# Gate masks and weights on GpSimd, a mixed pair turned by feature halves, and new instruction orders on four engines

## The chip, the cores and the metric

One core of one Trainium2 chip runs the kernel. The metric is device microseconds of one execution; the median of three runs of the kernel before is 122.1 us.

## The reference

`x` is (32, 32, 512) float32: 32 samples of 32 tokens (channels) with 512 features. Two residual blocks follow each other.

```python
# block 1
att   = softmax(gelu(gelu(cond @ W0 + b0) @ W1 + b1) @ W2 + b2)          # (32, 8)
mixed = einsum('boi,bih->boh', einsum('bk,koi->boi', att, weight), x) + (att @ bias_k)[:, :, None]
q, k, v = bitnet_linear(mixed, ...)         # sign of the weight times a row scale, nan_to_num
out   = softmax(q k^T / 4) v                # 32 heads of 16, 8 key/value heads, 32 keys
x     = x + bitnet_linear(out, o_weight, o_scale)
# block 2
y      = conv1d(x, weight(32, 8, 9), groups=4) + cond @ c_weight.T + bias
logits = y @ router_w.T + router_b          # 8 experts
w      = the two largest probabilities, divided by their sum, scattered into (N, 8)
x      = x + einsum('ner,eor->no', einsum('nd,erd->ner', y, A) * w[:, :, None], Bm) * 0.5
```

## The kernel before

The 1024 rows (sample, token) are eight tiles of 128 rows and four pairs of tiles. All engines run at once, each through a written-out list of small functions; semaphores join them, and an engine that meets a wait holds everything behind it in its list.

For pair `i`: VectorE makes the mixing matrices (`mix_weights`, `sum_weights`), TensorE mixes (`mix_bias`, `mix`), VectorE turns the result (`turn_mixed(i)`, two transposes, one for each tile of the pair) and makes its low part (`low_part(i, b)`, `b` a half of the features), ScalarE its high part (`high_part(i, b)`), TensorE projects to queries, keys and values (`project_first` for pair 0, `project(i, b)` after), ScalarE scales (`scale_qkv`), VectorE guards (`guard_qkv`) and turns the values. For tile `t` and head half `h`: GpSimd spreads keys and values block-diagonally (`spread_keys`, `spread_values`), TensorE scores, VectorE takes maxima and shifts (`row_tops`, `shift_rows`), ScalarE exponentiates, VectorE sums and inverts, GpSimd multiplies (`normalise(t, h)`), TensorE turns (`turn_probs`), ScalarE copies (`copy_probsT`), TensorE attends and projects out (`attend`, `project_out`), VectorE scales (`scale_y`), GpSimd adds the residual (`residual(t)`, VectorE for tile 7), ScalarE issues the store to DRAM (`store_x1(t)`), and SyncE reads it back as a shifted window (`to_window(t)`). Then TensorE convolves and turns (`convolve`, `turn_conv`), VectorE adds the bias (`bias_conv`), TensorE multiplies by the expert and router matrix (`ffn_up(t)`).

The gate of tile `t`: VectorE adds the router bias and finds the two largest logits with their indices (`gate_top`, L1006 to L1011), makes the indices floats and compares them with 0 to 7 (`gate_masks`, L1015, L1017), ScalarE makes the exponential of the difference (`gate_exponent`), VectorE makes its sum with one, the weights `gate_w` and the inverse (`gate_weights`, L1024, L1026, L1029), and applies them (`gate_apply`, L1035). TensorE turns (`turn_gated`), ScalarE copies (`copy_gatedT`), TensorE multiplies down (`ffn_down`), VectorE finishes (`finish`, L1047), SyncE stores.

Beside these, `o_scales` (VectorE) makes the output scales, SyncE stores them to DRAM and spreads them back (`store_o_scale`, `spread_o_scale`), `sum_o_scales` (ScalarE) waits for that, `bound_on_output` (GpSimd, five 1x1 operations) waits for the sum, and `bound_o` (VectorE) loads the flag. `keep_busy` is a matmul whose result nobody reads.

Of the kernel before, what the change touches and what calls it, by code (L numbers as in the profile page):

```python
# [10 lines left out]
ALU = mybir.AluOpType  # L11
# [3 lines left out]
P = 128  # L15
# [49 lines left out]
def build(nc, cond_pack, misc, mix_w, mix_b, x_rows, qkvT, qkv_rows, woT, wo_rows, conv_w,  # L65
          ffn_in, ffn_out, out):
    with ExitStack() as ctx:
# [299 lines left out]
        def _(pool):  # L367
# [103 lines left out]
            spread_keys(1)  # L471
            clear_windows()
            spread_keys(2)
            normalise(0, 0)
            spread_keys(3)
            spread_values(0)
            normalise(0, 1)
            normalise(1, 0)
            spread_values(1)
# [3 lines left out]
            bound_on_output()  # L483
            spread_keys(5)
            normalise(2, 1)
            residual(0)
            normalise(3, 0)
            spread_values(2)
            spread_values(3)
            spread_keys(6)  # L490
            normalise(3, 1)
            normalise(4, 0)
            residual(1)
            clear_third()
            gather_taps()
            spread_values(4)
            spread_keys(7)
            normalise(4, 1)
            normalise(5, 0)
            residual(2)  # L500
            residual(3)
            normalise(5, 1)
            spread_values(5)
            normalise(6, 0)
            normalise(6, 1)
            normalise(7, 0)
            spread_values(6)
            spread_values(7)
            residual(4)
            residual(5)  # L510
            normalise(7, 1)
            residual(6)


        @block.scalar
        def _(act):
# [51 lines left out]
            def high_part(i, b):  # L568
                act.wait_ge(mixed_turned, 2 * i + 2)
# [62 lines left out]
            def gate_exponent(t):  # L632
                act.wait_ge(top_ready, t + 1)
                nc.scalar.activation(gate_e[:, t % 2, :], logit_top[:, t % 2, 0:1], ACT.Exp, bias=logit_top[:, t % 2, 1:2],
                                     scale=-1.0).then_inc(gate_exp, 1)
# [6 lines left out]
            turn_shares()  # L642
            sign_qkv(0)
            sign_qkv(1)
            sign_qkv(2)
            sign_qkv(3)
            high_part(0, 0)
            high_part(0, 1)
            sum_x(0)
            sum_x(1)  # L650
            high_part(1, 0)
            high_part(1, 1)
# [3 lines left out]
            sum_x(2)  # L656
            sum_x(3)
            scale_qkv(0, 0)
# [5 lines left out]
            sum_rows(BLOCKS + 0, 3)  # L664
            high_part(2, 0)
            high_part(2, 1)
            scale_qkv(1, 0)
            scale_qkv(1, 1)
            sign_wo(0)
            sum_rows(BLOCKS + 2, 4)  # L670
            sign_wo(1)
            scale_qkv(1, 2)
            scale_qkv(1, 3)
            scale_qkv(1, 4)
            scale_qkv(1, 5)
            exponents(0, 0)
            scale_qkv(2, 0)
            high_part(3, 0)
            scale_qkv(2, 1)
            high_part(3, 1)  # L680
            scale_qkv(2, 2)
            exponents(0, 1)
            exponents(1, 0)
            exponents(1, 1)
            scale_qkv(2, 3)
            scale_qkv(2, 4)
            keep_conv_bias()
            scale_qkv(2, 5)
            copy_probsT(0, 0)
            exponents(2, 0)  # L690
            copy_probsT(0, 1)
            sign_wo(2)
            exponents(2, 1)
            scale_qkv(3, 0)
            scale_qkv(3, 1)
            sign_wo(3)
            attn_high(0)
            copy_probsT(1, 0)
            sum_o_scales()
            copy_probsT(1, 1)  # L700
            exponents(3, 0)
            exponents(3, 1)
            scale_qkv(3, 2)
            scale_qkv(3, 3)
            scale_qkv(3, 4)
            scale_qkv(3, 5)
            copy_probsT(2, 0)
            store_x1(0)
            attn_high(1)
            copy_probsT(2, 1)  # L710
            exponents(4, 0)
            exponents(4, 1)
            copy_probsT(3, 0)
            attn_high(2)
            copy_probsT(3, 1)
            exponents(5, 0)
            store_x1(1)
            copy_probsT(4, 0)
            exponents(5, 1)
            attn_high(3)  # L720
            copy_probsT(4, 1)
            exponents(6, 0)
            exponents(6, 1)
            store_x1(2)
            attn_high(4)
            store_x1(3)
            copy_convT(0)
# [943 lines left out]
```

## Time and profile before

| | us |
|---|---|
| three runs | 121.7, 122.1, 124.11 |
| profiled execution, its own time | 121.39 |
| span of the profiled execution | 119.6 |
| busy: TensorE, VectorE, ScalarE, GpSimd | 105.5, 92.7, 62.7, 48.9 |
| idle of TensorE until the scores of the first conditioning layer, and from its last matmul on | 2.75, 3.2 |

The span lies inside the execution's own time and is 1.8 us shorter. The busy time of TensorE counts the drain of a matmul, so a wait shorter than that drain does not show as idle.

### The profile page before, as it was taken

How to read it: one execution, taken by the hardware profiler on the slowest of the kernel's cores; microseconds unless marked ns; L12 is line 12 of the kernel's file. 1: busy time of each engine (PE TensorE's matmuls, PEld its weight loads, DVE VectorE, ACT ScalarE, POOL GpSimd, SP SyncE). 2: the span in 40 equal slices, each digit the busy share in tenths (PEclk: the TensorE clock that was granted, in tenths of full speed). 3: DMA queues.
4: the chain of work that ended last, by engine and by line, in shares of the span. 5: the costliest groups of instructions: out<-in, count | busy, mean ns of one | idle time of the engine just before them, and what ended most of it. 6: DMA issues, size and time to landing. Idle time of an engine off the chain costs nothing. (4 is left out here: it accounts for less than half of the span.)

```text
span 119.6 us, 3340 instructions
## 1 busy us (share of the span) xinstructions
PE 105.5 (88%) x1264; PEld 78.0 (65%) x1264; DVE 92.7 (77%) x244; ACT 62.7 (52%) x138; POOL 48.9 (41%) x74
## 2 busy tenths in 40 slices
PE   0979999979999899996869999899999899988870
PEld 0766698769999798974748577475756645644510
DVE  0158998839989999959989999979757685857851
ACT  4549889967484859395646163735244004031400
POOL 1020910025018639879999939693721000000000
PEclk9999999999999999999999999999999999999999
DMA  3899999950000000200393883997299859997032
GB/s 86 262 313 413 427 374 428 401 181 3 0 5 1 0 0 0 93 0 30 119 196 104 172 180 121 212 189 144 88 256 194 130 194 212 189 258 289 35 134 103
DMA packets 19237, 19.54 MB, mean 163 GB/s; under 512 B 1684, under 2 KB 14868, under 8 KB 18836
## 3 DMA queue, kind: packets, MB, share of 16 engines
q1 hardware_dynamic: 18068, 17.22, 55.7%
q10 hardware_dynamic: 1152, 2.10, 4.8%
q8 instruction: 10, 0.16, 0.6%
q14 instruction: 7, 0.06, 0.2%
HBM read 15.12 MB, written 4.20 MB: 162 GB/s over the span
## 5 line engine op out<-in xcount | busy, mean ns | idle before, releaser
L434 POOL TENSOR_TENSOR probs<-probs,row_inv 128x512 f32<-128x512 f32 x16 | 16.8, 1052 | 5.3 <-DVE row_inv L970 3.8
L1321 PE MATMUL halves<-mixed_hi,qkv_sign 128*128 128x256 f32 x72 | 17.3, 285 | 0.0
L1322 PE MATMUL halves<-mixed_lo,qkv_sign 128*128 128x256 f32 x72 | 16.7, 277 | 0.0
L1321 PEld LDWEIGHTS halves<-mixed_hi,qkv_sign 128*128 128x128 f32 x72 | 13.5, 188 | 0.4 <-issue 0.2
L1399 PE MATMUL halves<-wo_sign,attn_hi 128*128 128x512 f32 x32 | 13.6, 425 | 0.0
L1322 PEld LDWEIGHTS halves<-mixed_lo,qkv_sign 128*128 128x128 f32 x72 | 13.5, 188 | 0.0
L416 POOL TENSOR_TENSOR keys_diag<-kv,keymask 128x512 f32<-128x512 f32 x8 | 8.8, 1107 | 10.9 <-DVE calm L935 10.7
L1399 PE MATMUL halves<-wo_sign,attn_lo 128*128 128x512 f32 x32 | 12.6, 392 | 0.0
L966 DVE TENSOR_REDUCE row_sum<-probs 128x16 f32<-128x512 f32 x16 | 10.6, 671 | 1.5 <-ACT probs L590 1.4
L452 POOL TENSOR_TENSOR x_all<-x_all,o_out 128x512 f32<-128x512 f32 x7 | 9.0, 1280 | 6.3 <-DVE o_out L983 6.3
L590 ACT ACTIVATE probs<-probs 128x512 f32<-128x512 f32 x16 | 9.8, 628 | 3.3 <-DVE probs L960 3.3
L960 DVE TENSOR_TENSOR probs<-halves,row_max 128x512 f32<-128x512 f32 x16 | 10.6, 682 | 0.6 <-PE halves L1370 0.3
L954 DVE TENSOR_REDUCE row_max<-halves 128x16 f32<-128x512 f32 x16 | 10.2, 665 | 0.5 <-PE halves L1347 0.4
L1452 PEld LDWEIGHTS halves<-ffn_in_sb,woT_sb 128*128 128x128 f32 x64 | 8.1, 190 | 3.8 <-issue 2.8
L1465 PE MATMUL halves<-ffn_out_sb,gatedT 128*128 128x512 f32 x16 | 8.9, 641 | 1.3 <-ACT gatedT L640 0.7
L640 ACT ACTIVATE gatedT<-halves 128x128 f32<-128x128 f32 x8 | 2.2, 277 | 14.3 <-PE halves L1458 14.3
L1452 PE MATMUL halves<-ffn_in_sb,woT_sb 128*128 128x136 f32 x64 | 8.9, 285 | 0.7 <-ACT gatedT L640 0.5
L1347 PE MATMUL halves<-keys_diag,queries 64*128 64x128 f32 x128 | 9.2, 282 | 0.1
L580 ACT ACTIVATE queries<-halves,scale_all 128x256 f32<-128x256 f32 x16 | 6.8, 469 | 3.4 <-PE halves L1322 3.4
L1347 PEld LDWEIGHTS halves<-keys_diag,queries 64*128 64x128 f32 x128 | 7.9, 188 | 1.0 <-issue 0.7
L1047 DVE SCALAR_TENSOR_TENSOR x_all<-halves,x_all 128x512 f32<-128x512 f32 x8 | 5.5, 688 | 3.9 <-PE halves L1465 3.9
L426 POOL TENSOR_TENSOR vals_diag<-values_t,valmask 128x512 f32<-128x512 f32 x8 | 8.4, 1059 | 0.0
(144 smaller groups left out, 223.4 us busy)
## 6 DMA issues: line engine op xcount, KB each, us to landing
rows_sb<-x_turned SPq DMA_DIRECT2D x18, 256.0 KB, 5.1
x_all<-in_x_rows SPq DMA_DIRECT2D x4, 512.0 KB, 9.1
x_turned<-x_all ACTq DMA_DIRECT2D x8, 256.0 KB, 2.5
out_rows<-x_all SPq DMA_DIRECT2D x8, 256.0 KB, 3.7
qkvT_sb<-in_qkvT SPq DMA_DIRECT2D x4, 384.0 KB, 5.9
rows_sb<-in_qkv_rows SPq DMA_DIRECT2D x1, 1536.0 KB, 9.8
qkv_sign<-x_turned SPq DMA_DIRECT2D x6, 256.0 KB, 5.2
rows_sb<-in_wo_rows SPq DMA_DIRECT2D x1, 1024.0 KB, 14.0
```

Source lines behind the costliest of these rows:

```text
L434: pool.tensor_tensor(probs[:, t % 2, h, :, :], probs[:, t % 2, h, :, :], row_inv[:, t % 2, h, :].unsqueeze(2).to_broadcast([P, HALF, TOKENS]),
L452: pool.tensor_tensor(x1[:, t, :], x_all[:, t, :], o_out[:, t % 2, :], ALU.add).then_inc(x1_ready, 1)
L590: nc.scalar.activation(probs[:, t % 2, h, :, :], probs[:, t % 2, h, :, :], ACT.Exp, scale=float(DIM) ** -0.5).then_inc(exp_ready, 1)
L954: v.tensor_reduce(row_max[:, t % 2, h, :], scores, AX_X, ALU.max).then_inc(max_ready, 1)
L960: v.tensor_tensor(probs[:, t % 2, h, :, :], scores, row_max[:, t % 2, h, :].unsqueeze(2).to_broadcast([P, HALF, TOKENS]), ALU.subtract).th ...
L966: v.tensor_reduce(row_sum[:, t % 2, h, :], probs[:, t % 2, h, :, :], AX_X, ALU.add).then_inc(sum_ready, 1)
L1321: mm(dst, w, mixed_hi[:, ph, cols(i % 2, PAIR)], start=(ph == 0 and n % 2 == 0), stop=False)
L1322: last = mm(dst, w, mixed_lo[:, ph, cols(i % 2, PAIR)], start=False, stop=(ph == PHASES - 1 and n % 2 == 1))
L1347: last = mm(ps_scores[h][:, s * P:(s + 1) * P], queries[rows, PER_TILE * t + s, :, :], keys_diag[rows, t % 2, s, :, :].rearrange("p g k -> ...
L1399: last = mm(ps_y[:, :], part[:, t % 2, j, :, :], wo_sign[:, j, :], start=(j == 0 and part is attn_hi), stop=(j == MEMBERS - 1 and part is ...
L1452: last = mm(ps_ffn(t)[:, 0:FFN_COLS], convT[t % 2][:, ph, :, :], ffn_in_sb[:, ph, :], start=(ph == 0), stop=(ph == PHASES - 1))
L1465: mm(ps_down[:, :], gatedT[:, t % 2, :], ffn_out_sb[:, :], start=True, stop=True).then_inc(ffn_done, 1)
```

## The change

Four things change. (1) `gate_masks(t)` moves to GpSimd and becomes four operations: indices to float, a mask for the first index, a mask for the second times `gate_e`, and their sum `gate_w`. VectorE keeps the sum and the inverse; `gate_apply` waits for GpSimd's `gate_w`. (2) `turn_mixed(i)` makes its two transposes by halves of the features instead of by tiles, and `high_part(i, b)` waits for its own half alone. (3) Some waits protect the shared buffers (`idx_f_ready` before `max_index`, `gate_mask_ready` before the exponential, `gated_ready` before `gate_w`). (4) The lists of TensorE, VectorE, ScalarE and GpSimd are in new orders; SyncE's is the same.

```diff
+            def gate_masks(t):
+                iota = misc_sb[:, MISC["iota"]]
+                pool.wait_ge(gate_idx_ready, t + 1)
+                pool.tensor_copy(gate_idx_f[:, t % 2, :], gate_idx[:, t % 2, 0:2]).then_inc(idx_f_ready, 1)
+                pool.wait_ge(idx_f_ready, t + 1)
+                pool.tensor_scalar(gate_mask[:, t % 2, 0, :], iota, gate_idx_f[:, t % 2, 0:1], None, ALU.is_equal).then_inc(gate_mask_ready, 1)
+                pool.wait_ge(gate_exp, t + 1)
+                pool.tensor_scalar(gate_mask[:, t % 2, 1, :], iota, gate_idx_f[:, t % 2, 1:2], gate_e[:, t % 2, :],
+                                   ALU.is_equal, ALU.mult).then_inc(gate_mask_ready, 1)
+                pool.wait_ge(gate_mask_ready, 2 * (t + 1))
+                reached(pool, gated_ready, t - 1)
+                pool.tensor_tensor(gate_w[:, t % 2, :], gate_mask[:, t % 2, 0, :], gate_mask[:, t % 2, 1, :],
+                                   ALU.add).then_inc(gate_w_ready, 1)
             def high_part(i, b):
-                act.wait_ge(mixed_turned, 2 * i + 2)
+                act.wait_ge(mixed_turned, 2 * i + b + 1)
             def turn_mixed(i):
-                for a in range(2):
-                    v.transpose(mixed[:, i % 2, :, cols(a, P)].rearrange("p k (q o) -> p q k o", q=PER_TILE),
-                                mixing(i)[:, :, cols(a, P)].rearrange("p q (k r) -> p q k r", k=PHASES)).then_inc(mixed_turned, 1)
+                for b in range(2):
+                    v.transpose(mixed[:, i % 2, 2 * b:2 * b + 2, :].rearrange("p k (a q o) -> p q a k o", a=2, q=PER_TILE),
+                                mixing(i).rearrange("p q (a k r) -> p q a k r", a=2, k=PHASES)[:, :, :, 2 * b:2 * b + 2, :]
+                                ).then_inc(mixed_turned, 1)
```

The parts of the new lists that matter below, in their order:

```
GpSimd   ... normalise(1,0) bound_on_output spread_values(2) normalise(1,1) spread_keys(4) ...
         ... residual(4) gate_masks(0) normalise(7,0) normalise(7,1) residual(5) gate_masks(1)
         gate_masks(2) residual(6) gate_masks(3) ... gate_masks(7)
ScalarE  turn_shares sum_x(0) sign_qkv(0) high_part(0,0) high_part(0,1) sign_qkv(1..3) sum_x(1) ...
         ... scale_qkv(1,0) scale_qkv(1,1) sum_rows(6) sum_rows(8) scale_qkv(1,2) ...
         ... copy_probsT(0,0) scale_qkv(2,4) scale_qkv(2,5) sum_o_scales copy_probsT(0,1) scale_qkv(3,0) ...
         ... copy_gatedT(1) gate_exponent(2) store_x1(6) copy_gatedT(2) copy_convT(3) store_x1(7) ...
VectorE  ... turn_mixed(2) low_part(1,0) sum_scales keep_scale_v low_part(1,1) bound_qkv sum_rows(7)
         guard_qkv(0) sum_rows(9) turn_mixed(3) low_part(2,0) o_scales row_tops(0,0) ...
         ... finish(3) bias_conv(6) bias_conv(7) finish(4) gate_top(6) gate_weights(6) gate_apply(6)
         finish(5) gate_top(7) gate_weights(7) gate_apply(7) finish(6) finish(7)
TensorE  ... turn_shares keep_busy(1) mix_bias(0) mix(0) mix(1) keep_busy x3 mix_bias(1) keep_busy(1) mix(2) mix(3)
         ... score(2) turn_probs(0,1) project(3,0) attend(0) score(3) turn_probs(1,0) project(3,1)
         turn_probs(1,1) project_out(0) turn_probs(2,0) score(4) attend(1) turn_probs(2,1) project(3,2)
         score(5) turn_probs(3,0) attend(2) turn_probs(3,1) project_out(1) attend(3) turn_probs(4,0) ...
         ... ffn_up(1) turn_probs(7,0) attend(6) turn_probs(7,1) turn_gated(1) convolve(3) attend(7)
         project_out(6) ffn_down(0) ffn_up(2) project_out(7) turn_conv(3) turn_gated(2) ffn_down(1)
         ffn_up(3) convolve(4) convolve(5) turn_conv(4) turn_conv(5) turn_gated(3) ffn_down(2) ...
```

Before, `o_scales` stood behind `row_tops(1,1)`, `sum_o_scales` behind `copy_probsT(1,0)`, `low_part(1,0)` behind `mix_weights(3)`, `attend(0)` behind `project(3,1)`, `project(3,2)` ahead of `turn_probs(1,1)`, `turn_gated(1)` behind `turn_conv(2) project_out(6) turn_probs(7,1)`, `residual(6)` was GpSimd's last, `store_x1(6)` stood behind `copy_gatedT(2)`, and `ffn_down(1)` between `convolve(5)` and `turn_conv(4)`.

## Rows read from the trace of the kernel before

**Rows 1.** Part 1 of the page: busy time, share, instructions.
```profile
PE 105.5 (88%) x1264; PEld 78.0 (65%) x1264; DVE 92.7 (77%) x244; ACT 62.7 (52%) x138; POOL 48.9 (41%) x74
```
**Rows 2.** Busy time in four stretches (length, each engine, clock, DMA share, GB/s).
```profile
25.00:46.00 21.00, 20.50 (x214) 19.40 (x213) 18.63 (x39) 13.64 (x31) 9.44 (x13) 1.00 0.05 12
46.00:72.50 26.50, 24.02 (x358) 18.29 (x357) 23.96 (x49) 15.02 (x30) 22.71 (x29) 1.00 0.43 101
72.50:95.00 22.50, 21.19 (x232) 14.05 (x229) 17.67 (x55) 9.73 (x21) 11.86 (x11) 1.00 0.94 177
95.00:117.20 22.20, 19.08 (x123) 9.86 (x123) 15.94 (x63) 4.99 (x15) 0.00 (x0) 1.00 0.73 179
```
**Rows 3.** Waits of TensorE: total us, times, longest.
```profile
PE halves L1370 <- POOL probs L434: 1.6, 2, 1.3
PE halves L1370 <- ACT probsT L597: 1.0, 1, 1.0
```
**Rows 4.** Groups by line: total busy us, mean ns.
```profile
L828 DVE STREAM_TRANSPOSE mixed<-halves 128x512 f32<-128x512 f32 x8 | 5.2, 687 | 1.0 <-PE halves L1289 1.0
L946 DVE STREAM_TRANSPOSE values_t<-kv 128x128 f32<-128x128 f32 x4 | 1.2, 288 | 0.0
```
**Rows 5.** Timeline of the head: start us, length us.
```profile
8.60 1.24 PE L1280 MATMUL halves<-attT,mix_b_wide 32*128 32x256 f32 x8 [0.27 <-ACT attT L544]
11.22 1.65 PE L1235 MATMUL halves<-cond_sb 128*128 128x128 f32 x6
...
23.01 0.68 DVE L834 TENSOR_TENSOR mixed_lo<-mixed,mixed_hi 128x512 fp32r<-128x512 f32 x1
```
**Rows 6.** Timeline of the output scales: SyncE's queue, ScalarE.
```profile
37.42 0.38 SPq L321 DMA_DIRECT2D o_scale_row<-scale_all  x1
46.47 0.33 SPq L326 DMA_DIRECT2D o_scale_bc<-o_scale_row  x1
50.43 0.63 ACT L606 ACTIVATE junk_o<-o_scale_bc 1x512 f32<-1x512 f32 x1 [1.02 <-DMA o_scale_bc<-o_scale_row]
```
**Rows 7.** Timeline of TensorE: `turn_probs(0,1)`, then `project(3,1)`, then `attend(0)`.
```profile
43.65 0.60 PE L1360 MATMUL halves<-misc_sb,probs 128*128 128x128 f32 x4
...
46.02 1.08 PE L1386 MATMUL halves<-probsT,vals_diag 64*32 64x128 f32 x32
```
**Rows 8.** Timeline of GpSimd in `bound_on_output`, each operation waiting for the last.
```profile
51.59 0.19 POOL L444 TENSOR_TENSOR bound<-bound 1x1 f32<-1x1 f32 x1
51.85 0.18 POOL L446 TENSOR_TENSOR bound<-bound 1x1 f32<-1x1 f32 x1
```
**Rows 9.** Timeline of VectorE in the gate of tile 7, and the end.
```profile
112.73 0.17 DVE L1006 TENSOR_TENSOR logits<-halves,misc_sb 128x8 f32<-128x8 f32 x1 [0.20 <-PE halves L1452]
...
113.41 0.17 DVE L1015 CAST gate_idx_f<-gate_idx 128x2 f32<-128x2 uint32 x1
...
114.21 0.35 DVE L1035 SCALAR_TENSOR_TENSOR gated<-halves,gate_inv,gate_w 128x128 f32<-128x128 f32 x1
...
116.48 0.69 DVE L1047 SCALAR_TENSOR_TENSOR x_all<-halves,x_all 128x512 f32<-128x512 f32 x1 [1.32 <-PE halves L1465]
```
**Rows 10.** Timeline of GpSimd and of VectorE in the gate of tile 0.
```profile
80.44 1.31 POOL L452 TENSOR_TENSOR x_all<-x_all,o_out 128x512 f32<-128x512 f32 x1
80.71 1.05 DVE L1015 CAST gate_idx_f<-gate_idx 128x2 f32<-128x2 uint32 x1
```
**Rows 11.** Timeline: `residual(6)`, `store_x1(6)` and `(7)`, `ffn_up(3)`.
```profile
88.84 1.27 POOL L452 TENSOR_TENSOR x_all<-x_all,o_out 128x512 f32<-128x512 f32 x1 [2.26 <-DVE o_out L983]
94.86 1.75 ACTq L630 DMA_DIRECT2D x_turned<-x_all  x2
...
95.27 1.17 PE L1452 MATMUL halves<-ffn_in_sb,woT_sb 128*128 128x136 f32 x8 [0.46 <-ACT gatedT L640]
```
**Rows 12.** Timeline of GpSimd: the masks of the heads, each independent.
```profile
12.65 0.65 POOL L399 TENSOR_TENSOR keymask<-misc_sb 128x4 f32<-128x4 f32 x1
13.25 0.35 POOL L402 TENSOR_TENSOR valmask<-misc_sb 128x4 f32<-128x4 f32 x2
```

More of the change, by code:

```diff
@@ L642, in _ @@
             turn_shares()
+            sum_x(0)
             sign_qkv(0)
+            high_part(0, 0)
+            high_part(0, 1)
             sign_qkv(1)
@@ L1475, in _ @@
             turn_shares()
+            keep_busy(1)
             mix_bias(0)
@@ L1503, in _ @@
             project(1, 2)
+            conv_context()
+            score(1)
             project(2, 0)
-            score(1)
             project(2, 1)
             project(2, 2)
-            conv_context()
+            turn_probs(0, 0)
             score(2)
-            turn_probs(0, 0)
+            turn_probs(0, 1)
             project(3, 0)
-            turn_probs(0, 1)
-            project(3, 1)
             attend(0)
@@ L1516, in _ @@
             turn_probs(1, 0)
-            project(3, 2)
+            project(3, 1)
             turn_probs(1, 1)
             project_out(0)
+            turn_probs(2, 0)
             score(4)
-            turn_probs(2, 0)
             attend(1)
             turn_probs(2, 1)
+            project(3, 2)
+            score(5)
             turn_probs(3, 0)
-            score(5)
-            project_out(1)
             attend(2)
             turn_probs(3, 1)
+            project_out(1)
+            attend(3)
             turn_probs(4, 0)
+            project_out(2)
             score(6)
-            attend(3)
-            project_out(2)
+            turn_probs(4, 1)
             convolve(0)
-            turn_probs(4, 1)
-            project_out(3)
             attend(4)
             turn_probs(5, 0)
+            turn_conv(0)
+            project_out(3)
             score(7)
-            turn_conv(0)
-            project_out(4)
             turn_probs(5, 1)
@@ L1543, in _ @@
             turn_probs(6, 0)
+            turn_probs(6, 1)
             attend(5)
-            turn_probs(6, 1)
+            project_out(4)
             turn_conv(1)
             ffn_up(0)
+            convolve(2)
             project_out(5)
+            turn_gated(0)
+            turn_conv(2)
+            ffn_up(1)
+            turn_probs(7, 0)
             attend(6)
-            turn_probs(7, 0)
-            turn_gated(0)
-            convolve(2)
-            ffn_up(1)
-            turn_conv(2)
-            project_out(6)
             turn_probs(7, 1)
@@ L1559, in _ @@
             attend(7)
+            project_out(6)
+            ffn_down(0)
             ffn_up(2)
+            project_out(7)
             turn_conv(3)
-            ffn_down(0)
-            project_out(7)
             turn_gated(2)
+            ffn_down(1)
             ffn_up(3)
@@ L1567, in _ @@
             convolve(5)
-            ffn_down(1)
             turn_conv(4)
+            turn_conv(5)
             turn_gated(3)
-            turn_conv(5)
             ffn_down(2)
@@ L1574, in _ @@
             ffn_up(5)
+            ffn_down(3)
             convolve(6)
-            ffn_down(3)
             turn_gated(4)
+            turn_gated(5)
+            ffn_down(4)
             turn_conv(6)
-            ffn_down(4)
+            convolve(7)
             ffn_up(6)
-            convolve(7)
-            turn_gated(5)
             turn_conv(7)
```

293 lines of the change are left out of this document (140 added, 153 removed).

## The prediction

> **What bounds the kernel now.** I read the busy shares first: TensorE is busy for 88% of the span and VectorE for 77% [rows 1]. A share is an average, so the stretches come next [rows 2]. From 25 to 46 us TensorE idles 0.5 us in 21, and VectorE 2.4. From 46 to 72.5 us TensorE idles 2.5 us in 26.5, VectorE as much, GpSimd 3.8: three engines are near their limit at once, and any hand-over can stall the next. From 72.5 to 95 us TensorE idles 1.3 us, VectorE 4.8. From 95 us on, TensorE idles 3.1 in 22.2 us and VectorE 6.3: there the latency of one tile's chain counts, not throughput. So the most that new orders can win is what TensorE idles: 7.4 us in these four stretches. The waits say where some of it sits: two for GpSimd's `normalise`, 1.6 us together, one for ScalarE's `copy_probsT`, 1.0 us [rows 3]. The chain that ended last could be followed for 2.5% of the span only, so I walked each engine's new list by hand, each step as long as its row, and noted at marks how late TensorE is against before for the same work done. The profiled execution took 121.39 us, 0.7 below the median of 122.1; the sum is made against it, and I keep its 1.8 us outside the span.
>
> **Head, +0.6 us at `project(1,0)`.** The feature halves let `high_part(0,0)` start one transpose (0.69 us, rows 4) earlier. That wins nothing: `project_first` stands behind `mix(3)` in TensorE's list. If the new pattern of the transposes ran at the rate of the 128x128 one, a quarter of the size in 0.29 us, one would take 1.15 instead of 0.69, eight of them 3.7 us of VectorE [rows 4]. I take 0.69, because the nearest row is the same operation on the same 128x512 elements out of the same banks; the bounds are 0 and +3.7. One `keep_busy` now stands between `turn_shares` and `mix_bias(0)`, one between `mix_bias(1)` and `mix(2)`. Three of them took 1.65 us, so each is 0.55 [rows 5]. The first fills a wait of 0.27 us that TensorE had there [rows 5] and costs the rest, 0.28. The second replaces one that stood between `mix(3)` and `project_first`: nothing. Then `low_part(1,0)` (0.68 us, rows 5) stands in VectorE's list ahead of `keep_scale_v`, in place of two small sums of some 0.1 each that move away; `total_bound` waits for `keep_scale_v`, and `mix(6)`, `project(1,0)` stand behind it: half of the difference is covered by `mix_bias(3)`, +0.3. ScalarE does `sum_x(0)` while it would otherwise wait for weights, and comes to `scale_qkv(0,0)` 1.7 us later; its consumers have 2 us. Nothing.
>
> **Output scales, +1.15 us at `attend(0)`.** `o_scales` moves up, from 37.3 to 31.2 us by my walk (it needs `sum_rows(6)` and `(8)` of ScalarE, which follow `project(1,0)`). Its way through DRAM is long: 9.05 us from the first issue to the second [rows 6], and 3.96 more to ScalarE's sum [rows 6], 13.0 in all. It comes back at 44.3. But `sum_o_scales` moves up too, ahead of `copy_probsT(0,1)`, and ScalarE's list stops there. The sum (0.63 and an accumulator read) and the copy (0.6) end at 45.8, and `attend(0)` needs the copy. TensorE is there at 44.65, because `project(3,1)` is no longer ahead of `attend(0)`; before, that project and a `turn_probs` filled 2.4 us [rows 7]. It waits 1.15 us. Behind ScalarE's stopped instruction stand `scale_qkv(3,0)` and `exponents(2,0)` as well. Lateness now 1.75. This stall can be from 0 (if the DMA is 1.2 us faster) to 2.2 us (if the scales are 1 us later).
>
> **The middle, -1.95 us up to `score(7)`.** `project(3,2)` now comes behind `turn_probs(2,1)`, and `score(5)` ahead of `turn_probs(3,0)`: that is work in the place where TensorE waited 1.3 and 1.0 us [rows 3]. My walk finds each `normalise`, each copy and each key spread ready when TensorE comes, but five of them by 0.3 us or less. I take all of that gain, 1.95 us of the 2.5 that stand there [rows 2]; the bounds are 0 and 2.5. TensorE is then 0.2 us ahead of before.
>
> **Gate on GpSimd.** On VectorE three operations go: from the cast to `gate_apply` was 0.80 us [rows 9], of which the sum and the inverse stay, so about 0.45 us of its time for each tile, 3.6 us in all. VectorE had idle time in those stretches [rows 2], so this is worth little in itself. GpSimd's small dependent operations start 0.26 us apart [rows 8]. Four, with the hand-over both ways, make 1.15 us from index to `gate_apply` instead of 0.80: +0.35 us of latency per gate, 2.3 from the logits to `turn_gated` instead of 1.9. In the masks of the heads single GpSimd operations lasted 0.65 [rows 12]; with that price the four take 2.6 us and a gate +1.8. I take 0.26, the row with dependent operations of a few elements; the bounds are 0 (the operations overlap) and +1.8.
>
> One more row speaks for the change: in the gate of tile 0 the cast took 1.05 us instead of 0.17, and ended with GpSimd's `residual` of 80.44 us [rows 10]. That 0.9 us goes with the cast, but VectorE waited for nothing that TensorE needed at once, so I count it at nothing. The Trainium skill ("SBUF — State Buffer", Who interferes with whom) says that a cast can take the port pair that VectorE shares with GpSimd, and that whichever started first blocks the other fully; the row agrees, 80.71 + 1.05 = 81.76 against 80.44 + 1.31 = 81.75. The Trainium skill ("GPSIMD Engine Reference", Engine selection) advises against GpSimd for two-input elementwise work, as about twice as slow; by that rule the three moved operations would cost some 0.6 us more per gate, an estimate, instead of 0.35, and with it at the same three places the sum would end 0.7 higher.
>
> Where the latency shows. `turn_gated(1)` had `turn_conv(2)`, `project_out(6)` and `turn_probs(7,1)` between it and its `ffn_up`; now two turns and one `attend`, 1.45 us of work against 2.3 of latency: +0.85. In the remainder of that stretch the walk is 0.05 better, lateness 0.6 at the end of `project_out(7)`. Next, `residual(6)` now stands behind `gate_masks(2)` in GpSimd's list. Before it was done at 90.1 [rows 11]; now it waits for the indices of tile 2 and ends 3.1 us after `ffn_up(2)`, at 95.9. `store_x1(6)` waits for it, and behind it in ScalarE's list stand `copy_gatedT(2)` and `copy_convT(3)`, which `ffn_up(3)` needs: a wait of 0.7 us, in place of the 0.46 it had [rows 11] less what the new order would have saved of it, +0.4. Lateness 1.0. The store itself goes from 94.9 [rows 11] to 95.95, still in time for `convolve(6)`. `convolve(5)` to `turn_conv(5)` loses its cover, `ffn_down(1)`: +0.3; up to `ffn_up(7)` the walk wins 0.15. Then the end: the last gate is 0.35 longer, and `gate_apply(6)`, held by `gate_masks(6)`, keeps `finish(5)` and `gate_top(7)` behind it in VectorE's list 0.6 us past the end of `ffn_up(7)`; before, `gate_top(7)` was there and waited for it [rows 9]. +0.95.
>
> **Sum.** 0.6 + 1.15 - 1.95 + 0.8 + 0.4 + 0.3 - 0.15 + 0.95 = +2.1. The last `finish` would start at 118.6 instead of 116.5 [rows 9]. 121.4 + 2.1 = 123.5 us.
>
> **The rivals.** *Even:* the output scales come back in time, or the last gates overlap better: without the 1.15 and half of the 0.95 it is 121.9; band 120.7 to 122.3. For it: that stall hangs on one DMA time seen once. *The orders pay:* no new stalls, and the waits of the tail go too: 0.6 of the head, less 2.5 of the middle and 0.5 of the wait at `ffn_up(3)`, less some VectorE time that matters: 121.4 - 2.4 = 119.0; band 118.4 to 120.4. For it: nearly every wait of rows 3 has its work moved. Against it: `store_x1(6)` and `turn_gated(1)`, whose places need no price. *Slower by the masks:* GpSimd's four operations take 0.65 each. A gate costs +1.8 instead of +0.35, 1.45 more, at `turn_gated(1)`, at `store_x1(6)` and in the last gate, three places that nothing covers: 123.5 + 4.3 = 127.8; band 125 to 128. It decides from about 0.4 us per operation. *Slower in the transposes or by missed hand-overs:* the five near ones miss by 0.3 each, or the transposes take part of their +3.7: 124.8 to 126.5. *The halves do nothing* is part of the forecast already.
>
> **How the numbers follow.** Forecast band (122.3 to 124.6): 0.42. Even: 0.25. The orders pay: 0.15. Masks: 0.12. Transposes and hand-overs: 0.06. The forecast is the likeliest. 2% is about what a measurement of this kernel can tell from no change: 119.7 and 124.5 around 122.1. Faster takes most of the third case, 0.13; slower the last two and a tenth of the forecast band, with a little of what lies over it, 0.24; within 2% the remaining 0.63. The range leaves out a tenth at each end: 120.0 to 126.0. The case bands of both signs hold most of the chance, so the likeliest's own range is 122.3 to 124.6.
>
> **What the profile after would show.** Right: ScalarE's `junk_o` waiting for `o_scale_bc` at about 44 us with TensorE's `attend(0)` idle before it; the cast and three operations in GpSimd's rows, 1.1 us from first to last; waits of TensorE at `turn_gated(1)` on `gated`; `store_x1(6)` near 96 us; `gate_top(7)` starting 0.6 us after `ffn_up(7)`; the two waits of rows 3 gone. Wrong: transposes of over 0.8 us; GpSimd masks of 0.65; `attend(0)` without a wait; or TensorE stalls between 46 and 72 us, which would mean that my walk, with five hand-overs within 0.3 us, was too kind.

## The result, and the profile after

Four executions of the changed kernel took 125.64, 126.54, 124.47 and 123.58 us, median 125.06; four of the kernel before beside them had a median of 122.01. The ratio is 1.0163, 95% interval 1.0124 to 1.0203: slower, by 2.0 us. Ratios leave out executions more than 1.5% above the fastest of their kernel, here two of the four, while medians are of all, so the two need not agree. In a second measurement, beside three of the experiments, the median was 125.29 against 121.59, ratio 1.027 [1.0217, 1.0323], from five executions of six. The sign is the same in both; the sizes are 1.6 and 2.7%, and the first rests on two executions.

The profiled execution took 125.64 us with a span of 123.7. First the busy shares and the granted clock of its page.

```profile
PE 108.1 (87%) x1264; PEld 79.0 (64%) x1264; DVE 89.0 (72%) x220; ACT 62.6 (51%) x138; POOL 57.8 (47%) x106
...
PEclk9999999999999999999999999999999999999955
```

Against [rows 1] VectorE has lost 3.7 us of work and 24 instructions, GpSimd has won 8.9 us and 32. The last two slices run at half of the clock, of which more below. Next come the same four stretches as in [rows 2].

```profile
25.00:46.00 21.00, 19.86 (x242) 18.22 (x241) 19.55 (x44) 15.18 (x38) 11.24 (x16) 1.00 0.10 28
46.00:72.50 26.50, 25.83 (x380) 20.64 (x380) 24.75 (x55) 16.86 (x32) 22.82 (x27) 1.00 0.41 91
72.50:95.00 22.50, 20.11 (x218) 13.48 (x214) 15.03 (x41) 8.13 (x17) 12.12 (x20) 1.00 0.82 162
95.00:117.20 22.20, 18.76 (x130) 9.60 (x129) 12.60 (x46) 5.41 (x15) 6.63 (x22) 1.00 0.80 183
```

The first number is the length, the second TensorE's busy time; their difference is its idle time. Before it was 0.5, 2.5, 1.3 and 3.1 us; now it is 1.1, 0.7, 2.4 and 3.4, and the span ends 4.1 us later. The middle has won 1.8 us, and the stretches around it have lost more. (A stretch of time doesn't hold the same work in both kernels; a comparison of the same work follows the experiments.) The waits of TensorE say to what.

```profile
PE halves L1463 <- DVE gated L1048: 2.0, 4, 1.0
PE halves L1375 <- ACT probsT L619: 1.1, 2, 0.9
...
PE halves L1457 <- ACT woT_sb L643: 0.9, 1, 0.9
PE halves L1365 <- ACT probsT L623: 0.8, 1, 0.8
PE halves L1420 <- DMA rows_sb<-x_turned: 0.6, 1, 0.6
```

The two waits of [rows 3] are gone. In their place stand `turn_gated` waiting for `gate_apply` (four times, up to 1.0 us), `turn_probs(6,1)` and `turn_probs(7,1)` each behind a copy of ScalarE, `ffn_up(3)` behind `copy_convT(3)`, and `convolve(1)` behind its window. None of the four is `turn_gated(1)`. The chain of the page that ended last gives TensorE 54% of the span, VectorE 18%, DMA 9%, GpSimd and ScalarE 4% each: no single culprit.

The groups of VectorE show the new transposes, 694 ns each instead of the 687 of [rows 4].

```profile
L851 DVE STREAM_TRANSPOSE mixed<-halves 128x512 f32<-128x512 f32 x8 | 5.2, 694 | 2.1 <-PE halves L1294 2.1
```

The timeline, place by place (start, length, engine; the idle time before it in brackets): the output scales and `attend(0)`; `residual(6)`, `turn_gated(2)`, `store_x1(6)`, `ffn_up(3)`; and the gate of tile 7 to the end.

```profile
30.95 0.38 SPq L321 DMA_DIRECT2D o_scale_row<-scale_all  x1
...
40.47 0.33 SPq L326 DMA_DIRECT2D o_scale_bc<-o_scale_row  x1
...
44.68 0.63 ACT L628 ACTIVATE junk_o<-o_scale_bc 1x512 f32<-1x512 f32 x1 [1.88 <-DMA o_scale_bc<-o_scale_row]
...
45.98 0.67 PE L1391 MATMUL halves<-probsT,vals_diag 64*32 64x128 f32 x32 [0.45 <-issue]
...
95.22 1.27 POOL L466 TENSOR_TENSOR x_all<-x_all,o_out 128x512 f32<-128x512 f32 x1
...
95.70 0.33 PE L1463 MATMUL halves<-misc_sb,gated 128*128 128x128 f32 x1 [0.22 <-DVE gated L1048]
...
96.51 0.33 ACTq L652 DMA_DIRECT2D x_turned<-x_all  x1
...
97.76 0.50 PE L1457 MATMUL halves<-ffn_in_sb,woT_sb 128*128 128x136 f32 x2 [0.86 <-ACT woT_sb L643]
...
115.39 0.15 DVE L1030 TENSOR_TENSOR logits<-halves,misc_sb 128x8 f32<-128x8 f32 x1
...
116.08 0.19 POOL L453 CAST gate_idx_f<-gate_idx 128x2 f32<-128x2 uint32 x1 [1.60 <-DVE gate_idx L1036]
...
116.37 0.31 POOL L455 TENSOR_SCALAR gate_mask<-misc_sb,gate_idx_f 128x8 f32<-128x8 f32 x1
116.66 0.40 POOL L457 TENSOR_SCALAR gate_mask<-misc_sb,gate_idx_f,gate_e 128x8 f32<-128x8 f32 x1
117.15 0.20 POOL L461 TENSOR_TENSOR gate_w<-gate_mask 128x8 f32<-128x8 f32 x1
117.38 0.35 DVE L1048 SCALAR_TENSOR_TENSOR gated<-halves,gate_inv,gate_w 128x128 f32<-128x128 f32 x1 [0.93 <-POOL gate_w L461]
...
117.79 0.33 PE L1463 MATMUL halves<-misc_sb,gated 128*128 128x128 f32 x1 [1.04 <-DVE gated L1048]
...
118.48 2.07 PE L1470 MATMUL halves<-ffn_out_sb,gatedT 128*128 128x512 f32 x2 [0.37 <-ACT gatedT L663]
120.59 0.69 DVE L1060 SCALAR_TENSOR_TENSOR x_all<-halves,x_all 128x512 f32<-128x512 f32 x1 [2.26 <-PE halves L1470]
```

Read the gate first. From the cast to `gate_apply` it is 1.30 us where VectorE took 0.80 [rows 9]; GpSimd's three followers start 0.29, 0.29 and 0.49 us behind one another, and VectorE waits 0.93 us for `gate_w`. `ffn_up(7)` had ended at 114.77; its logits are read at 115.39 only, because `gate_apply(6)` and `finish(5)` stood ahead. The last `ffn_down` takes 2.07 us; with the full clock it takes 1.12 (below). The cast of tile 0, blocked for 0.9 us before [rows 10], is now on the engine that had blocked it and takes 0.19 (at 80.99 us).

### The profile page after: what moved, and what is told of

Its sections match the earlier page's. It is cut to its first block, busy times and chain, and to the rows that moved or that the text cites. A ratio compares the mean times of both kernels' runs of the same rounds, so it can differ in the third digit from the quotient of the medians.

```text
span 123.7 us, 3366 instructions
## 1 busy us (share of the span) xinstructions
PE 108.1 (87%) x1264; PEld 79.0 (64%) x1264; DVE 89.0 (72%) x220; ACT 62.6 (51%) x138; POOL 57.8 (47%) x106
## 4 chain that ended last, share of the span: by engine, by line
PE 54%; DVE 18%; DMA 9%; issue 6%; POOL 4%; ACT 4%; SPq 1%; ACTq 0%; POOLq 0%; DVEq 0%
PE halves L1404 8%; PE halves L1308 5%; PE halves L1352 5%; DMA qkv_sign<-x_turned 4%; PE halves L1420 4%; PE halves L1470 4%; PE halves L1294 4%; PE halves L1457 4%; DMA x_turned<-x_all 3%; PE halves L1326 3%; PE halves L1327 3%; PE halves L1285 3%; DVE mixed_lo L858 3%; DVE row_max L978 3%; DVE probs L984 3%
## 5 line engine op out<-in xcount | busy, mean ns | idle before, releaser
L1326 PE MATMUL halves<-mixed_hi,qkv_sign 128*128 128x256 f32 x72 | 17.7, 289 | 0.2 <-DVE mixed_lo L858 0.2
L453 POOL CAST gate_idx_f<-gate_idx 128x2 f32<-128x2 uint32 x8 | 1.5, 186 | 21.8 <-DVE gate_idx L1036 21.5
L426 POOL TENSOR_TENSOR vals_diag<-values_t,valmask 128x512 f32<-128x512 f32 x8 | 8.9, 1114 | 4.9 <-DVE values_t L972 4.3
L1470 PE MATMUL halves<-ffn_out_sb,gatedT 128*128 128x512 f32 x16 | 9.5, 677 | 1.1 <-ACT gatedT L663 1.1
L619 ACT ACTIVATE probsT<-halves 128x512 f32<-128x512 f32 x8 | 4.8, 597 | 7.2 <-PE halves L1375 5.8
```

The costliest lines, as they stand in the source:

```text
L426: pool.tensor_tensor(vals_diag[:, t % 2, :, :, :].rearrange("p s a (b d) -> p (s a) b d", d=DIM), values.unsqueeze(2).to_broadcast([P, 2 * ...
L1326: mm(dst, w, mixed_hi[:, ph, cols(i % 2, PAIR)], start=(ph == 0 and n % 2 == 0), stop=False)
L1470: mm(ps_down[:, :], gatedT[:, t % 2, :], ffn_out_sb[:, :], start=True, stop=True).then_inc(ffn_done, 1)
```

## The experiments

The forecast was a sum of stalls by place. Two ways of reading the result are to be told apart. One: the two parts, orders and masks, add up, and the masks cost where a gate's latency is bare. The other: each stall of the new orders that the trace shows costs its own length, so mending it gives that length back. Ratios are to the kernel before, in executions of the same chip.

**The masks alone.** The orders, transposes and lists of before; only `gate_masks` goes to GpSimd.

```diff
 residual(4)                      # GpSimd's list of before
+gate_masks(0)
 residual(5)
 normalise(7, 1)
+gate_masks(1)
 residual(6)
+gate_masks(2) ... gate_masks(7)
```

> The kernel before in its own orders, with only the gate's masks and weights on GpSimd. Theory M (the masks' latency is the cost): each gate 0.35 us longer, at the last gate and wherever nothing covers it, so 0.4 to 1.5 us slower than before (ratio 1.003 to 1.012), the four GpSimd operations about 1.1 us from first to last. Theory O (the new orders are the cost, the masks are harmless or help by the 0.45 us per tile that VectorE gains): within 0.3 us of before, or up to 1 us faster.

Median 123.95 us, ratio 1.0177 [1.0122, 1.0232]. Waits of VectorE and of TensorE in its trace:

```profile
DVE gated L1047 <- POOL gate_w L461: 5.7, 6, 1.0
```
```profile
PE halves L1462 <- DVE gated L1047: 1.4, 2, 1.0
```

The first line is the new one: 0.95 us of VectorE at each of six gates. The masks alone make the kernel slower, by 2.1 us, more than the 0.4 to 1.5 that were expected. Its trace also holds a wait of 1.97 us and a fall of the clock at 58 to 63 us, ahead of the first gate, which the masks can't have made.

**The orders alone.** The changed kernel with `gate_masks` and `gate_weights` on VectorE as before.

```diff
             gate_top(7)          # VectorE's list of after
+            gate_masks(7)
             gate_weights(7)      # and so for each tile
```

> The changed kernel with the masks back on VectorE, just ahead of gate_weights; halves and new orders stay. Theory M: most of the loss is gone, ratio to before 0.99 to 1.005. Theory O: it stays slow, 1.01 to 1.02, with store_x1(6) about 1.2 us earlier (residual(6) no longer behind the masks of tile 2) but with the waits for the output scales at attend(0) and for the windows as they are.

Median 123.03 us, ratio 1.0082 [1.0033, 1.0131]: the orders alone lose 1.0 us, between what the two theories expected. Its last gate, to be held against the one above:

```profile
115.14 0.17 DVE L1016 CAST gate_idx_f<-gate_idx 128x2 f32<-128x2 uint32 x1
...
115.95 0.35 DVE L1036 SCALAR_TENSOR_TENSOR gated<-halves,gate_inv,gate_w 128x128 f32<-128x128 f32 x1
```

0.81 us from the cast to `gate_apply`. 1.8% and 0.8% make 2.6%: what the second measurement of the changed kernel gave (2.7%), and more than the first did (1.6%).

**The halves alone.** The kernel before with the new `turn_mixed` and `high_part`.

> The kernel before with only the transposes of a mixed pair split by feature halves, and each high part waiting for its own half. Forecast of the record: nothing is gained, since project_first stands behind mix(3); the transposes last 0.69 us as before: ratio 0.997 to 1.003. Rival: the new pattern is slower (over 0.8 us each), which gives 1.005 or more; or the high parts that start 0.65 us earlier save time at project(1,0), 0.995 or less.

Median 121.83 us of 12 executions, ratio 1.0022 [0.9994, 1.0050]. The transposes by their group:

```profile
L828 DVE STREAM_TRANSPOSE mixed<-halves 128x512 f32<-128x512 f32 x8 | 5.2, 689 | 1.6 <-PE halves L1290 1.6
```

689 ns: the pattern is free, and the earlier start wins nothing that the runs can tell.

**A busy tail.** The changed kernel with nine matmuls that nobody reads around the last two gates, to hold the clock.

```diff
 turn_gated(6)
+stay_busy(2)
 ffn_down(6)
+stay_busy(5)
 turn_gated(7)
+stay_busy(2)
 ffn_down(7)
```

> The changed kernel with nine matmuls that nobody reads between the last turns and the last ffn_down, where TensorE waits for the gates. Theory C (in the changed kernel the clock falls to half in the last 5 us in some executions, because TensorE waits longer there, and this costs about 1 us when ffn_down(7) takes 2.08 instead of 1.12 us): the granted clock stays at 1.0 to the end in every execution, no execution of 125 us and over, median 123.5 to 124. Rival (the fall is not tied to what TensorE does in the tail): the low clock shows again in some executions, and the added matmuls change nothing or cost 0.2 us.

Median 125.06 us, ratio 1.0323 [1.0276, 1.0369]. The last `ffn_down`:

```profile
118.39 1.12 PE L1475 MATMUL halves<-ffn_out_sb,gatedT 128*128 128x512 f32 x2
```

The granted clock was 1.0 to the end and the matmuls took 1.12 instead of 2.07 us, but so they did without the filler in every other trace, the changed kernel's second one among them. The fall ahead of the last `ffn_down` belongs to that one execution and explains 0.95 us of its span. The expectation failed: two of the six executions had a mean clock of 0.984 and 0.985 in spite of the filler, three took over 125 us, and one of those, of 125.99 us, had the full clock. So the clock doesn't explain the median.

**The scales' sum later.** `sum_o_scales` behind `attn_high(0)` on ScalarE, `bound_on_output` behind `normalise(2, 0)` on GpSimd: the stall that the forecast priced highest is taken away.

```diff
 scale_qkv(2, 5)
-sum_o_scales()
 copy_probsT(0, 1)
 ...
 attn_high(0)
+sum_o_scales()
```

> The changed kernel with sum_o_scales back behind attn_high(0) in ScalarE's list and bound_on_output behind normalise(2,0) in GpSimd's. The record's step: ScalarE stopped for the output scales holds attend(0); in the trace of the changed kernel TensorE stood there about 0.45 us. Theory S (that stall carries to the end): the wait before attend(0) goes, 0.4 to 1.1 us faster than the changed kernel, ratio to before 1.007 to 1.013. Theory A (later waits, for the window of tile 1 and for copies of probsT, absorb it): attend(0) starts 0.4 us or more earlier, but the ratio stays at 1.014 to 1.019.

Median 125.15 us, ratio 1.0318 [1.0276, 1.0359]. TensorE and VectorE in its timeline:

```profile
44.91 0.67 PE L1391 MATMUL halves<-probsT,vals_diag 64*32 64x128 f32 x32
46.26 0.90 PE L1352 MATMUL halves<-keys_diag,queries 64*128 64x128 f32 x11 [0.69 <-DVE calm L959]
...
53.28 0.69 DVE L1007 TENSOR_TENSOR o_out<-halves,o_scale_bc 128x512 f32<-128x512 f32 x1 [1.43 <-POOL safe_flag L448]
...
57.33 0.94 PE L1352 MATMUL halves<-keys_diag,queries 64*128 64x128 f32 x12 [0.59 <-DVE probs L984]
```

`attend(0)` starts without a wait, 1.1 us earlier than in the changed kernel's trace; 0.6 of that is this execution's head (`project(1,0)` at 25.39 instead of 25.96), and 0.5 is the wait. But `score(3)` right behind waits 0.69 us for VectorE (by the profile, for `guard_qkv(1)`). The two lines below are from the busy tail, whose lists up to there are those of the changed kernel.

```profile
45.48 0.67 PE L1396 MATMUL halves<-probsT,vals_diag 64*32 64x128 f32 x32
46.83 1.16 PE L1357 MATMUL halves<-keys_diag,queries 64*128 64x128 f32 x16 [0.68 <-DVE calm L959]
```

There too `attend(0)` doesn't wait, and so in every trace of the new orders but the changed kernel's first. `score(3)` starts 20.86 to 20.99 us behind `project(1,0)` in all of them, with that stall (20.86) and without. So the stall cost nothing, because VectorE's work for `score(3)` ends last. The edit isn't a clean test of the rest, though: `bound_on_output` comes later with it, VectorE waits 1.43 us for its flag, and `score(5)` waits 0.59 us for VectorE. From `project(1,0)` to `project_out(3)` the three kernels with this edit take 44.1 us, the other traces of the new orders 43.2 to 43.4: the edit costs 0.8 us of its own.

**`residual(6)` first.** It goes ahead of `gate_masks(2)` in GpSimd's list.

> The changed kernel with residual(6) ahead of gate_masks(2) on GpSimd. The record's step: residual(6) behind the masks stops ScalarE at store_x1(6), and ffn_up(3) waits. Theory S: ffn_up(3) no longer waits 0.86 us for copy_convT(3), 0.5 to 0.9 us faster than the changed kernel, ratio to before 1.009 to 1.012. Theory A (the rest is bound by the gates' latency, so the time comes back as waits for the gates): the wait goes but the ratio stays at 1.014 to 1.019.

Median 124.86 us, ratio 1.0286 [1.0244, 1.0328]. Timeline of TensorE at `ffn_up(3)`:

```profile
97.85 1.20 PE L1457 MATMUL halves<-ffn_in_sb,woT_sb 128*128 128x136 f32 x8
```

The wait of 0.86 us is gone: from `ffn_up(2)` to `ffn_up(3)` it takes 4.73 us instead of 5.61. The time is no better than the changed kernel's by more than the runs can tell (124.9 against 125.1). But the trace says what became of the gain: it is still there at the last gate (`turn_gated(2)` and `turn_gated(7)`).

```profile
96.67 0.33 PE L1463 MATMUL halves<-misc_sb,gated 128*128 128x128 f32 x1 [0.21 <-DVE gated L1048]
...
117.86 0.33 PE L1463 MATMUL halves<-misc_sb,gated 128*128 128x128 f32 x1 [1.04 <-DVE gated L1048]
```

That is 21.2 us from the one to the other, where the changed kernel takes 22.1 (95.70 to 117.79). What this execution won there it had lost before: `project_out(4)` ran at half of the clock and took 3.3 us instead of 2.1. Four of the six executions had a mean clock as low as this one's (0.975 to 0.977); whether that ate the gain in them too isn't shown.

**All mended, with either engine for the masks.** The head's `keep_busy` as before, both edits above, `residual(2)` ahead of `spread_values(5)`, and `attend(5)` between `turn_probs(6,0)` and `(6,1)`; once with the masks on GpSimd, once on VectorE.

> The changed kernel with five places mended: the two keep_busy back where they were, sum_o_scales and bound_on_output as in e5, residual(6) as in e6, residual(2) ahead of spread_values(5), and attend(5) between turn_probs(6,0) and turn_probs(6,1). If the stalls that the orders make are what costs: about 2 us faster than the changed kernel, ratio to before 0.995 to 1.005. If GpSimd's gate latency is what costs: still 1.008 to 1.015, with the last gates unchanged (0.9 us of VectorE idle before gate_apply(7)).

> The same five places mended in the kernel with the new orders and the masks on VectorE (residual(6) needs none there). If both the orders' stalls and GpSimd's latency cost, this is the fastest: ratio to before 0.985 to 1.0. If the mends win nothing because later waits absorb them, it stays at the 1.008 of the orders alone.

Masks on GpSimd: median 125.74 us, ratio 1.0321 [1.0268, 1.0374]. On VectorE: 123.54 us, 1.0174 [1.0135, 1.0213]. Neither is better than its parent (125.1 and 123.0), and the second is worse than the orders alone (1.0082, in another set of executions) by more than the intervals. Between the two the ratios differ by 1.5%, 1.8 us, again for the masks. The traces say why nothing came back: the edit for the sum costs its 0.8 us in both (`score(5)` waits 0.66 and 0.64). In the first, the 0.9 us of `residual(6)` are won, but `convolve(2)` waits 1.8 us for its window, and `project_out(5)` behind it takes 3.4 us at half of the clock. The late window isn't new with these edits: it cost 1.3 us in the orders alone and 1.55 with the head restored.

**The changed kernel again, and three more.** The first is the second measurement quoted above. The tail on VectorE: tiles 3 to 7 have their masks and weights on VectorE, tiles 0 to 2 on GpSimd. The head restored: the three `keep_busy` where they were. The swap: `attend(5)` between the two `turn_probs` alone.

```diff
 gate_top(3)                      # VectorE's list, tiles 3 to 7
-gate_weights(3)
+tail_masks(3)                    # gate_masks as before, counted by two
+tail_weights(3)                  # gate_weights as before
```

> The changed kernel once more, beside the three others and the kernel before on one chip. If the ratio of the first measurement (1.016) holds, the part for the orders (0.8%) and the part for the masks (1.8% in before's orders) do not add up, or only partly. If those two parts add up, the ratio is 1.025 to 1.03, some 124.5 to 125 us, as the other versions built on it showed.

> The changed kernel with the masks and weights of tiles 3 to 7 made by VectorE again, those of tiles 0 to 2 still by GpSimd. Theory (latency of the last gates): from 95 us on each tile waits for its gate, so this takes back most of what the masks cost: 1.5 to 2 us less than the changed kernel, the last gate_apply some 0.5 us behind the index of tile 7 nearer to it (0.85 instead of 1.36), and no wait of VectorE on gate_w. Rival (the cost lies in the first gates and in GpSimd's residual and stores before 95 us): no more than 0.6 us less. Rival (the clock falls whenever TensorE has idled, whoever makes the masks): the time stays within 0.5 us.

> The changed kernel with the three keep_busy of the head back where they were before. The forecast priced them at 0.28 us at project(1,0). Theory: project_first and project(1,0) start 0.3 to 0.5 us earlier, and the gain is absorbed before 46 us by the wait for the output scales, so the time is within 0.3 us of the changed kernel. Rival: the head sets the pace of everything behind it, and the time falls by 0.5 us or more. Second rival: keep_busy in the wait holds the clock up, and without it the head gets slower, by 0.5 us or more.

> The changed kernel with attend(5) between turn_probs(6,0) and turn_probs(6,1) on TensorE, as cover for ScalarE's copy. The changed kernel idles 0.87 us there. Theory: that wait goes (0.6 to 0.9 us in place), and the chain of tiles 2 and 3 behind it, which waits for VectorE and ScalarE, takes most of it back: 0 to 0.4 us less. Rival: each idle of TensorE counts in full: 0.8 us less.

| | median us | ratio |
|---|---|---|
| again | 125.29 | 1.0270 [1.0217, 1.0323] |
| tail on VectorE | 124.83 | 1.0276 [1.0231, 1.0322] |
| head restored | 125.13 | 1.0270 [1.0223, 1.0316] |
| swap | 125.23 | 1.0187 [1.0138, 1.0236] |

The head restored: no gain, as the theory said, but not for its reason. `project(1,0)` doesn't start earlier; it starts 18.8 us behind `turn_shares`, against 18.2 in the changed kernel's first trace and 18.9 in its second. The swap: its median is the changed kernel's, and the means of the six executions are 125.0 and 125.2; its ratio is better, at the edge of the intervals, and I take it for no gain shown. With it `turn_gated(7)` starts at 117.91 us against 117.79. It is still the useful trace, since its clock stayed at 0.999: the timeline of its last two steps, then the same in the tail on VectorE.

```profile
113.79 1.09 PE L1457 MATMUL halves<-ffn_in_sb,woT_sb 128*128 128x136 f32 x8
...
117.91 0.33 PE L1463 MATMUL halves<-misc_sb,gated 128*128 128x128 f32 x1 [1.05 <-DVE gated L1048]
```
```profile
114.62 1.09 PE L1475 MATMUL halves<-ffn_in_sb,woT_sb 128*128 128x136 f32 x8
...
117.86 0.33 PE L1481 MATMUL halves<-misc_sb,gated 128*128 128x128 f32 x1 [0.55 <-DVE gated L1061]
```

From `ffn_up(7)` to `turn_gated(7)` it takes 4.12 us with GpSimd's masks and 3.24 with VectorE's; the orders alone had 3.17. So 0.9 us in the last gate is shown in place. But the time did not follow: 0.46 us of the medians and nothing of the ratio, where 1.5 to 2 were expected. In that trace `project_out(4)` took 3.4 us instead of 2.1, at half of the clock; of the other executions only the mean clock is recorded (0.985 to 1.0, 0.986 here).

**The same work in every trace.** From `turn_gated(2)` to `turn_gated(7)` all kernels do the same work on TensorE, and behind `turn_gated(7)` each trace has 4.98 us left (the changed kernel's first has 5.93, by the fall of its clock). First the two ends in the kernel before, then, with `ffn_up(3)` between them, in the orders alone.

```profile
94.54 0.27 PE L1458 MATMUL halves<-misc_sb,gated 128*128 128x128 f32 x1
...
114.62 0.33 PE L1458 MATMUL halves<-misc_sb,gated 128*128 128x128 f32 x1 [0.33 <-DVE gated L1035]
```
```profile
96.01 0.33 PE L1459 MATMUL halves<-misc_sb,gated 128*128 128x128 f32 x1 [0.15 <-DVE gated L1036]
...
97.19 1.19 PE L1453 MATMUL halves<-ffn_in_sb,woT_sb 128*128 128x136 f32 x8
...
116.36 0.33 PE L1459 MATMUL halves<-misc_sb,gated 128*128 128x128 f32 x1 [0.48 <-DVE gated L1036]
```

| us from start to start | `turn_gated(2)` to `ffn_up(3)` | to `ffn_up(7)` | to `turn_gated(7)` | all |
|---|---|---|---|---|
| before | 0.73 | 16.33 | 3.02 | 20.1 |
| masks alone | 0.73 | 16.99 | 3.77 | 21.5 |
| orders alone, and mended with VectorE's masks | 1.18 | 16.0 | 3.17 | 20.35 |
| changed kernel (twice), head restored, sum later, busy tail, swap | 2.06 | 15.9 | 4.11 | 22.1 |
| `residual(6)` first, and all mended | 1.18 | 15.9 | 4.10 | 21.2 |
| tail on VectorE | 2.06 | 16.45 | 3.24 | 21.75 |

Traces of one kind agree within 0.03 us here. The orders cost 0.3 us in this part, and the masks in the new orders 1.8: 0.9 at `ffn_up(3)`, because `residual(6)` stands behind `gate_masks(2)`, and 0.9 in the last gate. This also says why the tail on VectorE won little: it kept `residual(6)` behind `gate_masks(2)`, lost 0.5 us more in the middle column (`turn_conv(5)` and `turn_gated(4)` wait longer), and had only the last gate to win.

## Why the prediction was right

It gave 123.5 us, with 120.0 to 126.0 and the chance on "within 2%". Measured: 125.06 in the first set, a ratio of 1.016. The sign and the range hold, though the second measurement, 1.027, lies over 2%; the likeliest's own band of 122.3 to 124.6 was left by 0.5 us on the upper side. In the changed kernel's first trace, same work against same work, the parts of the sum come out so. (`score(3)` is compared without `project(3,1)`, 2.01 us, and `score(7)` without `turn_conv(0)`, 0.41, which the two lists put on different sides.)

| TensorE's lateness gained | forecast | measured |
|---|---|---|
| up to `project(1,0)` | +0.6 | +0.44 |
| to `score(3)` | +1.15 | +1.37 |
| to `score(7)` | -1.95 | -1.99 |
| to `turn_gated(2)` | +0.8 | +1.33 |
| to `turn_gated(7)` (0.4 + 0.3 - 0.15 + 0.95) | +1.5 | +2.01 |
| sum | +2.1 | +3.2 |

The middle was right, and the rest was priced low by 1.1 us in all. The forecast of 2.1 us agrees with the first measurement (2.0), but not with the second (3.3) nor with this sum, so the close fit to the first ratio is partly luck. By its steps:

- *Head, +0.6.* Measured 0.44 at `project(1,0)` (25.52 to 25.96 us), but that can't be told from chance: with the same head it starts 17.4 to 18.9 us behind `turn_shares` in eight traces, against 17.7 before. Restoring it gave nothing back, in place or in time.
- *Transposes.* 694 ns, as taken; the price of +3.7 us from the small pattern fell. The halves alone: 1.0022.
- *Output scales, +1.15 at `attend(0)`.* The stop of ScalarE is there: 13.7 us from the first issue (30.95) to the sum (44.68), forecast 13.0, and `attend(0)` at 45.98 against 45.8. But TensorE came 0.9 us later than in my walk and waited 0.45 instead of 1.15, in this trace and in no other. The lateness at `score(3)`, near the forecast in size, has another cause: `score(3)` waits for VectorE, with the stall at `attend(0)` or without it. The step was wrong in its mechanism, and its size came out near by luck.
- *Middle, -1.95.* 1.99 from `score(3)` to `score(7)`, TensorE's idle 0.7 instead of 2.5 us: right, and the largest term.
- *Gate, +0.35.* 0.50 measured (1.30 less 0.80, cast to `gate_apply`). The price of 0.26 us per operation came from a chain of 1x1 operations; here the cast of 128x2 and the first mask are followed after 0.29 each, and the operation that compares and multiplies after 0.49. The rival price of 0.65 fell. The three operations that left VectorE were busy 0.57 us there by the sum of their rows, and GpSimd's four are 1.10. The Trainium skill ("GPSIMD Engine Reference", Engine selection) has GpSimd about twice as slow for elementwise work with two inputs; 1.9 times is near that, but it compares four operations with three others, and the one two-input operation among GpSimd's took 0.20 us, so the rule itself isn't tested. The +0.6 worked out from it was nearer than my +0.35. The Trainium skill ("Perfetto Trace Analysis", GPSIMD Engine Instruction) says to time GpSimd by the spacing of starts and not by the spans; so read, the four steps from the cast make 1.30, where the spans sum to 1.10.
- *`turn_gated(1)`, +0.85.* The wait for the gate that this step forecast is not there: TensorE's wait on that row is 0.02 us, and at most 0.2 in any trace. `turn_probs(7,1)` just ahead of it waits 0.77 us for `copy_probsT`, and 0.58 in the orders alone, whose masks are VectorE's. So little of the lateness there is the masks'. The other lateness of this stretch comes from two hand-overs that the walk counted as met: `turn_probs(6,1)` straight behind `(6,0)` waits 0.9 for `copy_probsT`, `convolve(1)` 0.6 for its window.
- *`residual(6)` behind `gate_masks(2)`, +0.4.* As forecast to the place: ended 96.49, store at 96.51, `ffn_up(3)` waits 0.86 (0.7 forecast). Mended, it gives 0.9 us back as far as the last gate in both traces, though the times don't show it. The term was half of that.
- *End, +0.95.* `gate_top(7)` 0.62 us behind the end of `ffn_up(7)`, 0.6 forecast. The rest of the difference at `turn_gated(7)`, 117.79 where the sum gives 116.7 (114.62 + 2.1), is what came before plus the gate's 0.15. The last `finish` stood 0.95 us later again, by the clock of that execution.

So the terms that were mis-sized are those of the masks behind `turn_gated(2)`: they cost 1.8 us in place, half of it through `residual(6)` (0.9 for a term of 0.4) and half in the last gate (0.9 more than with VectorE's masks, where the latency alone was priced at 0.35). The step that was wrong in its mechanism is the output scales, and with it the forecast of a wait on the gate at `turn_gated(1)`. By the times the masks alone cost 2.1 us, and the ratios of the changed kernel and of the orders alone differ by 1.9%, 2.3 us. The orders alone lost 1.0. What the whole adds up to, 2.0 or 3.3 us, the two measurements leave open; the parts, and the traces with their 3.2, speak for the larger.

The walk by places treated each stall as lasting and as its own. The runs show two kinds. The stall at `attend(0)` cost nothing, since another wait ended later right behind it. The one at `ffn_up(3)` lasted to the end.

Not settled: the 0.5 to 0.9 us by which the times put the masks above what the traces show in place (1.8 in the new orders, 1.4 in those of before), and why the times of `residual(6)` first and of the tail on VectorE don't follow their traces. The falls of the clock in the middle of some executions are a candidate that no run tests. No version beat the kernel before, and the best of the changed ones, the halves apart, was the orders with VectorE's masks, 0.8% slower.

## What to carry to other kernels

Moving small dependent operations to an idle engine is paid in latency: 0.46 us of VectorE's busy time was freed per tile (3.7 us over eight), and the chain that everybody waited for became 0.5 us longer, in a stretch where VectorE idled anyway. The idle engine's own list counts too: a residual that stood behind the moved operations cost as much again. Count such a move by the chain's latency and by what queues behind it, and not by the busy shares. Before a stall is priced at its length, look at the next wait of the same engine: where that one ends later whatever you do, as at `score(3)`, the stall is worth nothing. And when times scatter by more than the effect, compare the time between the same two instructions, with the same work between them, in several traces; here it agreed within 0.03 us in six traces whose spans differ by up to 2.9.

## What was not expected of the hardware

The granted clock of TensorE fell from 2.4 to 1.2 GHz for a few microseconds in the middle of some executions, and matmuls took half as long again or more: `project_out` 3.55 us instead of 2.12 in the masks alone, 3.4 instead of 2.1 with the tail on VectorE, the last `ffn_down` 2.07 instead of 1.12 in the changed kernel. Five of the fourteen traces have such a fall between 58 and 87 us, each behind waits of TensorE. With `residual(6)` first the waits were those of `convolve(1)` and `turn_probs(6,1)`; the third line is the stretch behind them, granted clock 0.50:

```profile
72.86 1.07 PE L1420 MATMUL halves<-rows_sb,conv_w_sb 96*32 96x512 f32 x8 [0.77 <-DMA rows_sb<-x_turned]
...
75.19 0.46 PE L1375 MATMUL halves<-misc_sb,probs 64*128 64x64 f32 x8 [0.87 <-ACT probsT L619]
```
```profile
76.00:79.00 3.00, 3.00 (x30) 2.13 (x15) 1.77 (x4) 1.87 (x4) 1.11 (x2) 0.50 1.20 214
```

Such waits are not enough, though: the busy tail, whose lists are the same up to there, had nearly the same two, and kept the full clock.

```profile
73.34 1.07 PE L1425 MATMUL halves<-rows_sb,conv_w_sb 96*32 96x512 f32 x8 [0.74 <-DMA rows_sb<-x_turned]
...
75.67 0.46 PE L1380 MATMUL halves<-misc_sb,probs 64*128 64x64 f32 x8 [0.87 <-ACT probsT L619]
```
```profile
76.00:79.00 3.00, 3.00 (x49) 2.33 (x45) 2.37 (x6) 2.12 (x4) 1.63 (x2) 1.00 1.26 201
```

The profiled execution of before had a mean of 0.999. A kernel with more bare waits may meet such falls more often, which would be one more cost of the change; fourteen traces, one or two for each kernel, can't show that.
